# Another order of the same operations on TensorE, VectorE, ScalarE and GpSimd in a chunked scan-attention-expert kernel

## The reference, cut to what matters

```python
x = x + mamba(_layernorm(x))        # in-projection, conv, silu, then per channel and state:
#   s = clip(s * A + b_t * x_t, -10, 10); y = sum_n c_t * s     for 1024 time steps
#   out = (y * silu(z)) @ out_w.T + out_b + residual, layer norm
x = x + ffn(_layernorm(x))          # gate, top 2 of 8 experts: relu(x @ w1) @ w2, weighted by comb
x = x + performer(_layernorm(x))    # causal linear attention over prefix sums, then gelu MLP of 1024
x = x + ffn(_layernorm(x))          # the same experts again
```

## Time and profile before

| | |
|---|---|
| median of 3 runs | 1932.68 us (1932.35 to 1937.6) |
| the profiled execution, its own time | 1935.1 us |
| its span, first to last instruction | 1933.3 us, mean granted TensorE clock 0.956 |
| PE busy | 1824.8 us (94%) |
| PEld busy | 1548.2 us (80%) |
| DVE busy | 1589.3 us (82%) |
| ACT busy | 514.5 us (27%) |
| POOL busy | 238.2 us (12%) |
| chain that ended last | PE 80%, DVE 1%, issue 1% |
| copies of a chunk's scan output (L977), first and last | 231.0 and 1783.4 us, 16 of them |

### The profile page before, as it was taken

One profiled execution on the slowest core, in us unless ns is written; L12 is line 12 of the kernel. 1 busy time (PEld: TensorE's weight loads), 2 busy tenths in 40 slices (PEclk: granted clock), 3 DMA queues, 4 the chain that ended last, 5 costly groups with the idle time before them and its releaser, 6 DMA issues.

```text
span 1933.3 us, 57679 instructions
## 1 busy us (share of the span) xinstructions
PE 1824.8 (94%) x18048; PEld 1548.2 (80%) x18048; DVE 1589.3 (82%) x6006; ACT 514.5 (27%) x1121; POOL 238.2 (12%) x516
## 2 busy tenths in 40 slices
PE   6886578999999999999999999999999999999997
PEld 3444366988888888888898988888888888898886
DVE  4466887898989898989898998989898989898432
ACT  3342011313232322222232213132323222232322
POOL 0001110102020101011111111020202011111100
PEclk9885687999999999999999999999999999999998
DMA  6843010100001010101000101001010101010000
GB/s 216 280 138 94 19 30 9 30 15 25 25 20 29 16 30 20 30 20 30 20 25 16 34 15 29 21 19 31 15 30 20 30 20 30 21 30 9 2 7 6
DMA packets 101046, 72.71 MB, mean 38 GB/s; under 512 B 64905, under 2 KB 94625, under 8 KB 99745
## 3 DMA queue, kind: packets, MB, share of 16 engines
q1 hardware_dynamic: 98448, 67.30, 12.3%
q10 hardware_dynamic: 2320, 1.85, 0.3%
HBM read 45.50 MB, written 23.59 MB: 36 GB/s over the span
## 4 chain that ended last, share of the span: by engine, by line
PE 80%; DVE 1%; issue 1%; ACT 0%; DVEq 0%; POOL 0%; ACTq 0%
PE bank L1207 28%; PE bank L1194 23%; PE bank L1108 6%; PE bank L1123 5%; PE bank L1335 3%; PE bank L1282 3%; PE bank L1141 2%; PE bank L1296 1%; PE bank L1289 1%; PE bank L1269 1%; PE bank L1161 1%; PE bank L1315 1%; PE bank L1346 1%; PE bank L1325 1%; DVE x L1692 0%
## 5 line engine op out<-in xcount | busy, mean ns | idle before, releaser
L1574 DVE CUSTOM_DVE_ANT_0 state<-decayed_state,bank 128x128 f32<-128x128 f32 x2048 | 507.1, 287 | 53.8 <-PE bank L1108 41.9
L1564 DVE TENSOR_TENSOR decayed_state<-state,decay 128x128 f32<-128x128 f32 x2048 | 504.4, 287 | 2.7 <-issue 2.7
L1207 PE MATMUL bank<-f_w_sb,hs_whole 128*128 128x256 f32 x2048 | 486.6, 380 | 1.0 <-ACT hs_whole L1001 1.0
L1207 PEld LDWEIGHTS bank<-f_w_sb,hs_whole 128*128 128x128 f32 x2048 | 371.9, 190 | 49.6 <-ACT hs_whole L1001 5.8
L1001 ACT ACTIVATE hs_whole<-bank,f_b_sb 128x256 f32<-128x256 f32 x512 | 214.5, 471 | 647.4 <-PE bank L1194 647.4
L1108 PE MATMUL bank<-xrows,brows 128*128 128x256 f32 x1024 | 258.7, 343 | 46.4 <-DVE state L1574 34.9
L1108 PEld LDWEIGHTS bank<-xrows,brows 128*128 128x128 f32 x1024 | 174.8, 199 | 91.2 <-issue 46.1
L826 POOL TENSOR_TENSOR m_ve<-m_mv,m_eps 128x2 f32<-128x2 f32 x96 | 20.1, 209 | 1229.4 <-DVE m_mv L1606 1229.4
L1194 PE MATMUL bank<-fT_parts,f_w_hi 128*128 128x256 f32 x1024 | 170.1, 289 | 0.7 <-ACT fT_parts L971 0.7
L1194 PE MATMUL bank<-late_fT_parts,f_w_hi 128*128 128x256 f32 x1024 | 169.9, 289 | 0.0
L1123 PE MATMUL bank<-state,cblk 128*32 128x256 f32 x2048 | 147.2, 408 | 3.7 <-DVE state L1574 3.7
(11 more groups left out here) (160 smaller groups left out, 2353.9 us busy)
## 6 DMA issues: line engine op xcount, KB each, us to landing
brows<-bs_dram SPq DMA_DIRECT2D x1020, 2.0 KB
xrows<-xs_dram SPq DMA_DIRECT2D x480, 32.0 KB
xt<-in_x SPq DMA_DIRECT2D x4, 1024.0 KB, 8.0
xn_dram<-xn SPq DMA_DIRECT2D x4, 1024.0 KB, 5.4
z_dram<-zT SPq DMA_DIRECT2D x4, 1024.0 KB, 4.1
f_w_sb<-in_f_w SPq DMA_DIRECT2D x2, 2048.0 KB
xs_dram<-xhi SPq DMA_DIRECT2D x4, 1024.0 KB, 4.5
xs_dram<-xlo SPq DMA_DIRECT2D x4, 1024.0 KB, 8.7
```

The source lines that it names most:

```text
L1207: last = pe.matmul(bank_[:, tile * D:(tile + 1) * D], hs_whole[:, slot, m, tile * P:(tile + 1) * P], w(m), start=(m == 0 and tile == 0 and ...
L1564: dve.tensor_tensor(decayed_state[:, part], state[:, (s - 1) % RING, part], decay[:, part], ALU.mult).then_inc(decayed.sem, 1)
L1574: dve._custom_dve(add_sat, out=state[:, s % RING, part], in0=decayed_state[:, part], in1=U[s // 2 % 2][:, s % 2 * D + h * HALF:s % 2 * D + ...
```

## The change

Nothing is added, removed or computed otherwise. In the four `step` functions the calls stand in another order, for all rounds alike, and on PE four pairs of tile products come to stand next to each other that did not before: y(2) with y(3), new_states(0) with new_states(1), y(6) with y(7), y(5) with from_chunk(1). Two neighbourhoods are given up: from_chunk(0) with y(5), and new_states(1) with y(6). The diff, cut to the lines that the prediction speaks of:

```diff
 POOL
-                rstd_of(c, LN1)
-                add_mlp_bias()
...
                 rstd_of(c, LN2)
+                add_mlp_bias()
 ACT
-                spread_kv(c)
-                copy_hi(c, T_MLP)
-                copy_y(i)
-                gelu(c, 0)
+                copy_y(i)
+                copy_hi(c, T_MLP)
+                gelu(c, 0)
+                spread_kv(c)
 PE, head of a round
-                u(0)
-                u(1)
-                turn_y()
-                mlp_second(0)
-                mamba()
-                mlp_first(late, 1)
+                turn_y()
+                u(0)
+                mlp_first(late, 1)
+                mamba()
+                mlp_second(0)
+                u(1)
 PE, middle
-                y(2)
...
-                y(3)
...
+                y(2)
+                y(3)
                 u(17)
 PE, before the scores
                 features(g["wq"], q_made)
+                second_layer(late, 1, 3)
+                first_layer(late, 1, 4)
+                u(21)
                 turn_k()
+                u(22)
                 second_layer(late, 1, 4)
+                u(23)
                 y(4)
                 scores()
+                first_layer(late, 1, 5)
                 u(24)
                 u(25)
-                first_layer(late, 1, 5)
                 from_states()
 PE, end of a round
                 u(29)
                 new_states(0).then_inc(kv_half.sem, 1)
+                wait_apart(kv_half, kv_half.after(c, 1))
+                new_states(1).then_inc(kv_made.sem, 1)
+                u(30)
                 attention_out()
-                second_layer(late, 1, 6)
-                u(30)
                 first_layer(late, 1, 7)
-                wait_apart(kv_half, kv_half.after(c, 1))
-                new_states(1).then_inc(kv_made.sem, 1)
+                u(31)
+                second_layer(late, 1, 6)
                 y(6)
-                u(31)
+                y(OCTS - 1)
                 tpose_set(c, T_MLP, yl_done)
                 second_layer(late, 1, 7)
-                y(OCTS - 1)
                 mlp_first(c, 0)
 DVE, head of a round
-                scan(0, 1)
                 gate_y()
-                scan(1, 3)
+                scan(0, 2)
                 add_tokens()
                 ln_stats(c, MAMBA, res, h_done, (1, 1))
-                scan(3, 5)
+                scan(2, 4)
                 mamba_norm()
+                scan(4, 5)
                 ln_stats(c, FFN1, res, x1_done, (1, 2))
 DVE, before the masks
-                scan(43, 45)
                 add_expert(late, 1, 3, x3)
-                scan(45, 46)
-                query_feature(0)
-                query_feature(1)
+                scan(42, 45)
                 add_expert(late, 1, 4, x3)
-                scan(46, 48)
+                scan(45, 48)
                 mask(0)
                 mask(1)
                 mask(2)
 DVE, end of a round
-                scan(56, 60)
+                scan(56, 62)
                 add_attention()
                 ln_stats(c, LN2, a_t, xr_done, (1, 1))
-                scan(60, 62)
-                add_expert(late, 1, 6, x3)
+                scan(62, 64)
                 add_states()
-                scan(62, 64)
+                add_expert(late, 1, 6, x3)
                 low_half_mlp()
```

More of the change, by code:

```diff
@@ L1058, in step @@
                 relu(c, 0, 7)
+                copy_comb(late, 1)
                 relu(late, 1, 0)
@@ L1401, in step @@
                 first_layer(c, 0, 0)
+                u(6)
                 gate(c, 0)
                 first_layer(c, 0, 1)
+                u(7)
                 if_both(x3_done, late, 1)
                 second_layer(c, 0, 0)
[L1406 removed]
                 turn_comb(c, 0)
                 first_layer(c, 0, 2)
[L1409 removed]
+                u(8)
+                second_layer(c, 0, 1)
                 bias(c, 0)
[L1411 to L1412 removed]
+                u(9)
+                first_layer(c, 0, 3)
+                y(1)
+                second_layer(c, 0, 2)
+                u(10)
+                second_layer(c, 0, 3)
+                first_layer(c, 0, 4)
                 if_both(acc_set[0], c, 1)
                 tpose_set(late, T_FFN2, xf_done[1])
[L1415 to L1420, removed]
                 u(11)
[L1422 removed]
+                first_layer(c, 0, 5)
                 u(12)
                 second_layer(c, 0, 4)
[L1425 to L1427 removed]
+                gate(late, 1)
+                second_layer(c, 0, 5)
                 first_layer(c, 0, 6)
                 u(13)
[L1430 to L1431 removed]
                 first_layer(c, 0, 7)
                 second_layer(c, 0, 6)
[L1434 to L1435 removed]
+                u(14)
+                turn_comb(late, 1)
                 second_layer(c, 0, 7)
@@ L1438, in step @@
                 first_layer(late, 1, 0)
-                u(16)
-                y(2)
+                u(15)
+                if_both(relued[0], c, F // P * E)
+                first_layer(late, 1, 1)
                 if_both(acc_done[0], c, TILES * (E - 1))
                 second_layer(late, 1, 0)
-                if_both(relued[0], c, F // P * E)
-                first_layer(late, 1, 1)
+                u(16)
+                bias(late, 1)
+                first_layer(late, 1, 2)
+                y(2)
+                y(3)
                 u(17)
-                first_layer(late, 1, 2)
                 if_both(acc_done[0], c, TILES * E)
                 second_layer(late, 1, 1)
-                u(18)
-                first_layer(late, 1, 3)
                 if_both(acc_set[1], late, 1)
                 tpose_set(c, T_ATT, xl_done)
-                y(3)
[L1454 to L1457, removed]
+                second_layer(late, 1, 2)
+                u(18)
                 if_both(relued[1], late, F // P * 2)
@@ L1460, in step @@
                 features(g["wk"], k_made)
[L1461 to L1466, removed]
+                u(19)
+                values()
+                first_layer(late, 1, 3)
+                u(20)
                 pe.wait_ge(kT_done.sem, kT_done.after(c, 1))
                 features(g["wq"], q_made)
+                second_layer(late, 1, 3)
+                first_layer(late, 1, 4)
+                u(21)
                 pe.wait_ge(kT_done.sem, kT_done.after(c, 1))
@@ L1804, in step @@
-                low_half(c, T_FFN1)
+                scan(10, 12)
+                routing(c, 0)
+                scan(12, 16)
                 ln_stats(late, FFN2, x3, x3_done, (1, 1))
-                scan(10, 11)
-                routing(c, 0)
-                scan(11, 15)
+                scan(16, 17)
                 set_acc(c, 0, res, res)
-                scan(15, 16)
                 add_expert(c, 0, 0, res)
-                scan(16, 18)
+                scan(17, 18)
                 add_expert(c, 0, 1, res)
-                scan(18, 19)
+                scan(18, 20)
```

71 lines of the change are left out of this document (34 added, 37 removed).

## The result

The changed kernel takes 1968.5 us (median of 4 runs, 1965.2 to 1976.2) against 1932.5 for the kernel before: a ratio of 1.0188, 95% interval 1.0149 to 1.0227. It is slower by 36 us, where 1931 was forecast with a range to 1940. Its profiled execution took 1965.4 us, with a span of 1962.6, 29.3 more than before.

The account below looks back on a forecast made before the run. PE was taken to bound the fourteen loop rounds; per round -0.45, -0.48, +0.28 and +0.70 us sum to +0.05. With chunk 1 and the last steps at -1 us each: 1931 us, own range 1926 to 1937, reaching 1918 to 1940.

Parts of the forecast that it names:

- Chunk 1: Before the loop: steps 60 and 61 fill DVE's wait for attention_out, -1 us, with 3 either way.
- Term 1: Tile products next to each other on PE save ways in and out: y pair -0.31, new_states pair -0.14, together -0.45 a round.
- Term 2: PE waits that go: gelu at a round's head -0.28, y(4) -0.13, masks before from_states -0.07; -0.48 a round.
- Term 3: PE waits that come: late expert 4's relu +0.28, masks before from_states +0.70 a round.
- the second half waits for the completion of the first: Between new_states(0) and new_states(1), PE waits 0.20 us; pair net -0.14 a round, bounds -0.22 and +0.10.
- PE's other work is the same: In the sum over the rounds: PE's work outside the three terms was taken as unchanged, adding nothing.
- The last steps: After the loop: fewer relu and gelu waits, -1 us, with 2 either way.
- Rivals A and B: A: new waits covered, only savings stay, 1919 us, chance 0.29; B: ln_apply chain bounds a round's head, 1939 us, chance 0.17.
- The rule on tile modes: Changing tiling mode drains PE; counted so, 25 changes a round become 20, and the sum is some 0.15 lower a round.

Follow-up runs that it names:

- e3: Changed kernel with 127 more do-nothing instructions at PE's program start, shifting the loop's code half a block of 256; 1972.1 us, ratio 1.0185.
- e5: Changed kernel with its loop's code shifted 16 instructions further on by already met waits at PE's program start; 1966.2 us, ratio 1.0164.
- e8: Changed kernel with its loop's code shifted 240 instructions further on, so one block is exactly the new_states pair; one run, 1983.6 us.
- e4: Kernel before with 196 more do-nothing instructions at PE's program start, so one block holds 248 of the scores' 256 instructions; 1956.1 us, ratio 1.0102.
- e6: Kernel before with its loop's code shifted 128 instructions further on, no product moved; 1943.1 us, ratio 1.0047.
- e12: Changed kernel with the new_states halves apart and y(3) moved away from y(2), behind the transposes of T_ATT; one run, 1939.6 us.
- e1: Changed kernel with new_states(1) put back behind attention_out and first_layer 7, so the halves are apart; 1932.8 us, ratio to before 0.9997.
- e7: Changed kernel with the new_states halves apart and DVE's scan step 45 moved ahead of late expert 4's addition; 1934.0 us, ratio 1.0003.
- e11: Changed kernel with attention_out alone moved between the two halves of new_states; 1953.8 us, ratio 1.0106.
- e9: Changed kernel with the new_states halves apart and y(5) moved from between the two from_chunk to directly ahead of from_states; 1953.7 us, ratio 1.0097.

## Why the prediction was wrong

**The forecast's own terms were nearly right.** The one round of the changed kernel without a gap lasts 103.20, forecast 103.25, though in part because errors of 0.1 cancel. Chunk 1 came out 1.0 us shorter, as forecast, but that hit is within its scatter: with nothing but the place of the code changed it lasts 107.6 to 109.5 in the new order (e3, e5, e8) and 107.8 to 109.9 in the old (e4, e6). One sum in the prediction is off by 0.05: with all bounds at the upper end the round's change is +0.82, not +0.87; the forecast doesn't change by it.

- Term 1: two y's together cost 1.86, and e12 prices that at 0.30 (0.31 forecast). new_states with new_states was mis-sized: forecast at -0.14, of which 0.20 was the wait between the halves. From the first half's start to the second's it is 0.90, against 0.66, so 0.24. And with the halves apart and away from y(6) (e1) a round is shorter by 0.09 than in the round of the changed kernel that has no gap, so the pair brought nothing even there, as far as one round can tell.
- Term 2 gave 0.18 of its 0.28 at the head. The transposes' 0.18 is gone, but the other 0.10 only moved: mlp_second costs 1.54 and mamba, now the first of the two, 1.83, as it did the other way round before. In e1 gate_y ends at 1059.63 and mamba starts at 1059.69, so the slack that the prediction saw there ("gate_y, which ends about 1.9 behind the head, and PE is there at 2.1") is next to nothing. y(4)'s wait is hidden by u(23), but the scores themselves cost 1.69 instead of 1.52, which the wait for the masks covers.
- Term 3: the relu's wait came back as forecast (0.50 instead of 0.24 for the u, second_layer 1.64). At from_states PE waits 0.60 where 0.70 stood in the sum, for the masks, as forecast. These rows of the changed kernel show both:

```profile
1038.68 0.48 PE L1108 MATMUL bank<-xrows,brows 128*128 128x256 f32 x2
1039.19 1.99 PE L1207 MATMUL bank<-f_w_sb,hs_whole 128*128 128x256 f32 x8
...
1045.53 0.63 PE L1108 MATMUL bank<-xrows,brows 128*128 128x256 f32 x4
1046.59 1.17 PE L1325 MATMUL bank<-kv,qT 128*64 128x68 f32 x32 [0.43 <-DVE ss L1779]
```

**The step that failed** is in term 1: "the second half waits for the completion of the first", bounded at -0.22 and +0.10. I priced the pair by the array and by semaphores alone, at -0.14 a round and at most +0.10. What the runs show in its place is a stop of PE inside the pair, for code, of 1.11 us on the mean in thirteen of fourteen rounds, and a clock drop of 1.6 behind four of them: a round lasts 104.70 on the mean with the pair and 103.15 without it (e1). The pair is also 256 instructions that PE gets through in 1.4 us, and the row of before that would have warned me isn't a PE row at all but DMA queue 8 of kind "instruction", with ten packets a round that take 0.9 to 1.4 us each. Neither rival named it, nor the text's list of what would prove it wrong. "PE's other work is the same" was the sentence that hid it, and the clock, granted in full before, was taken as given.

**The last steps** were forecast at -1 us and came out at +8.6: the gap in mamba of 2.3 us, a clock drop behind it, and small waits that I didn't price one by one; with the halves apart they are +1.3 in e1, but +4.9 in e7 and +6.2 in e12, which has a gap of 1.93 us in the scores of the last steps. So this part isn't the pair's alone, and what decides it is open.

**Rivals A and B** did not occur. In the rounds no ln_apply ends a wait of PE.

**The rule on tile modes.** By the Trainium skill, page TensorEngine Tiling (Array Packing), section Tiling Modes, which the prediction set against the row, only new_states with new_states and y with y should be free. e12 bears out the y pair; for new_states the halves' own wait covers it, so no run here decides it.

Open: what makes a packet start at the pair and not 2 us earlier, since shifts of the edge by 0, 16 and 240 instructions gave about the same start; why the gap of e8 stands five matmuls early; and what decides whether the clock falls behind a gap (it fell behind gaps of 0.94 and not behind one of 1.51). Each of the five forecasts for shifted code missed in time, in place or altogether, so the place of a block's edge alone doesn't foretell the loss. No version beat both kernels: e1 and e7 equal the kernel before.

## What to carry to other kernels

Count instructions per microsecond as well as array time: a run of some 250 tiny matmuls and weight loads without long ones around it can outrun the arrival of its own code, and the profile then shows a gap of PE ended by "issue" at a fixed instruction, with a length that changes from round to round. It need not: the scores of the kernel before are as dense, and none of its rounds has a gap. Here 1.5 us of large products between the halves (e11) or 3 us (e1) were enough to end the gap. When rounds of the same loop differ in length, lay the packets of the instruction queue beside the gaps before looking at semaphores. Where a change may put an idle gap of a microsecond into a busy PE, add to the bound what the clock cost here: 1.6 us behind four of thirteen gaps.

## What the hardware showed that I had not expected

- A packet of code takes 0.9 to 1.4 us, and PE goes on only 1.2 to 1.6 us behind its end (1.7 to 1.9 at the loop's start in e3).
- The place of the code alone changes where PE stands still: with the same products in the same order, a shift by 16 instructions moves the gap by eight matmuls, one by 127 moves it from the pair to the loop's start.
- The clock can fall without any idle time of PE ahead of it (e9), and cost up to 3 us a round.
- A met wait with a no-op behind it isn't free on PE: its first product starts at 23.1 and 23.3 us with 128 and 129 of them (e3, e6), at 30.8 with 197 (e4) and at 35.6 with 241 (e8), against 13.0 without. The main part began 6 to 22 us later; its start scatters by 4.7 us between the kernels without them.
